# Order of VectorE's scores, sums, maxima and quantisation in a 16-head attention kernel

## What is computed

```python
xn = layernorm(x)                                   # over the last axis, no weights
q = heads(xn @ q_w.T + q_b) / 4;  k = heads(xn @ k_w.T + k_b);  v = heads(xn @ v_w.T + v_b)
ctx = softmax(q @ k.T) @ v                          # 16 heads, 4096 x 4096 scores each
attn = merge(ctx) @ out_w.T + out_b
ffn = ((fp8(xn * sx) @ fp8(w * sw).T) / (sx * sw) + bias).astype(bfloat16)   # e4m3, one scale each
out = x + attn + ffn
```

## Time and profile before

| | us |
|---|---|
| median of 3 runs (lowest, highest) | 2136.94 (2135.54, 2138.78) |
| profiled execution, its own time | 2133.51 |
| its span in the profile | 2131.7 |
| TensorE busy | 2010.7 |
| ScalarE busy | 1833.7 |
| VectorE busy | 1302.3 |
| mean granted TensorE clock | 0.973 of full |

### The profile page before, as it was taken

One profiled execution on the slowest core, in us unless ns is written; L12 is line 12 of the kernel. 1 busy time (PEld: TensorE's weight loads), 2 busy tenths in 40 slices (PEclk: granted clock), 3 DMA queues, 4 the chain that ended last, 5 costly groups with the idle time before them and its releaser, 6 DMA issues.

```text
span 2131.7 us, 39151 instructions
## 1 busy us (share of the span) xinstructions
PE 2010.7 (94%) x13433; PEld 661.4 (31%) x13433; DVE 1302.3 (61%) x1822; ACT 1833.7 (86%) x2004; POOL 32.2 (2%) x53
## 2 busy tenths in 40 slices
PE   6889999999999999999999999999999999999988
PEld 4523232322323232322323232222322232222327
DVE  6555566665555567655555667555555666565556
ACT  2259898998989898998989899998989899898973
POOL 2000000000000000000000000000000000000000
PEclk9989999999999999999999999999999999999999
DMA  6850201212020111111030111112020011111022
GB/s 204 265 193 9 42 10 15 27 23 28 13 37 8 30 14 20 28 22 28 8 42 8 17 26 22 28 23 28 8 42 8 15 27 23 28 21 29 8 38 80
DMA packets 65525, 82.12 MB, mean 39 GB/s; under 512 B 9952, under 2 KB 47360, under 8 KB 62208
## 3 DMA queue, kind: packets, MB, share of 16 engines
q1 hardware_dynamic: 65472, 81.58, 18.9%
HBM read 54.79 MB, written 26.21 MB: 38 GB/s over the span
## 4 chain that ended last, share of the span: by engine, by line
PE 74%; DVE 20%; issue 2%; DMA 2%; SPq 1%; ACT 0%; DVEq 0%; ACTq 0%
PE banks L1089 39%; PE banks L1063 29%; DVE d_probs L835 6%; DVE d_probs L831 3%; DVE bits L820 3%; DVE d_probs L838 2%; DVE bits L826 2%; PE banks L977 2%; DVE powers L823 2%; PE banks L1189 1%; PE banks L988 1%; PE banks L1021 1%; DMA k_parts<-probs 1%; DVE o_junk L640 1%; DVE qt L641 1%
## 5 line engine op out<-in xcount | busy, mean ns | idle before, releaser
L583 ACT ACTIVATE probs<-banks 128x1024 f32<-128x1024 f32 x1923 | 1783.1, 1179 | 159.2 <-PE banks L1063 154.4
L1089 PE MATMUL banks<-probs,v_st 128*32 128x512 f32 x7680 | 1036.8, 612 | 3.0 <-DVE o_sb L801 3.0
L1063 PE MATMUL banks<-q_st,k_st 50*128 50x512 f32 x4102 | 863.2, 471 | 25.3 <-DVE bits L820 18.9
L1063 PEld LDWEIGHTS banks<-q_st,k_st 50*128 50x128 f32 x4102 | 378.2, 186 | 1001.0 <-ACT probs L583 882.6
L835 DVE SCALAR_TENSOR_TENSOR d_probs<-d_probs,bits 128x1024 f32<-128x1024 f32 x256 | 313.6, 1225 | 8.8
L820 DVE TENSOR_SCALAR bits<-banks 128x512 int32<-128x512 f32 x256 | 177.1, 692 | 203.6 <-PE banks L1063 191.6
L1089 PEld LDWEIGHTS banks<-probs,v_st 128*32 128x32 f32 x7680 | 152.3, 108 | 291.1 <-issue 270.8
L801 DVE STREAM_TRANSPOSE o_sb<-banks 128x512 f32<-128x512 f32 x32 | 22.9, 717 | 357.3 <-PE banks L1089 357.3
L831 DVE SCALAR_TENSOR_TENSOR d_probs<-bits 128x1024 f32<-128x1024 f32 x128 | 156.9, 1225 | 13.0 <-PE banks L1089 9.8
L838 DVE SCALAR_TENSOR_TENSOR d_probs<-d_probs,powers 128x1024 f32<-128x1024 f32 x128 | 157.9, 1234 | 4.4
L826 DVE TENSOR_SCALAR bits<-bits 128x1024 int32<-128x1024 int32 x128 | 88.9, 695 | 4.4
(11 more groups left out here) (91 smaller groups left out, 483.4 us busy)
## 6 DMA issues: line engine op xcount, KB each, us to landing
k_st<-k_parts SPq DMA_DIRECT2D x204, 128.0 KB, 4.4
q_st<-q_parts SPq DMA_DIRECT2D x204, 64.0 KB, 5.1
q_parts<-probs SPq DMA_DIRECT2D x9, 512.0 KB, 6.1
k_parts<-probs SPq DMA_DIRECT2D x9, 512.0 KB, 6.2
xnT_copy<-probs SPq DMA_DIRECT2D x8, 512.0 KB, 4.4
probs<-xnT_copy SPq DMA_DIRECT2D x8, 512.0 KB, 8.0
w_f<-xnT_copy SPq DMA_DIRECT2D x16, 256.0 KB, 5.1
out_dram<-qt SPq DMA_DIRECT2D x16, 256.0 KB, 2.1
```

The lines of the kernel that those rows point to most:

```text
L583: act.activation(probs[:, at:at + WIDE * CHUNK].rearrange("p (t c) -> p t c", t=WIDE), banks[:, bank:bank + WIDE, :], ACT.Exp, scale=1.0 / ...
L1063: return pe.matmul(out, k_mm[rows, kt * P:(kt + 1) * P], blocks[rows, qb // GROUPS], start=True, stop=True)
L1089: last = pe.matmul(banks[VCOLS * qb:VCOLS * (qb + 1), 6, :], v_st[:, kt, :], tile, start=(pos == 0), stop=(pos == KT - 1), tile_position=( ...
```

## The change

It moves the slots of VectorE's scores and sums, puts a D row's sum behind the block's own sum of its round instead of between the round's two pairs, takes maxima over 32 keys (16 query tiles of 32 columns in one bank, made in two parts in slots 36 and 38 and reduced once), makes those scores from 48 rows instead of 16, moves the transposing matmul to slot 46, and puts quantisation behind the maxima on VectorE.

```diff
-    D_SLOTS = ((5, 6, 9, 16), (18, 25, 27, 34))
-    D_SUM = (26, 44)
+    D_SLOTS = ((2, 4, 6, 14), (16, 24, 26, 34))
+    D_SUM = (23, 43)
-    MAX_FIRST, MAX_TURN = 42, 47
+    MAX_SLOTS, MAX_TURN = (36, 38), 46
-    AK = 64
-    JT = CHUNK // AK
+    AK = CHUNK // UT
...
-                self.max_jobs = UT * (S // CHUNK) if full else UT // JT
+                self.max_jobs = UT * (S // CHUNK) if full else 1
...
-            if e in D_SUM:
-                SUM_ORDER.append((e, None, D_SUM.index(e), D_ROWS[D_SUM.index(e)]))
+            SUM_ORDER += [(e, None, d, D_ROWS[d]) for d in range(len(D_ROWS)) if D_SUM[d] == e]
...
-                def some_maxima(j, job0):
-
-                    dve.wait_ge(c.misc_full, job0 + (j + 1))
-                    dve.tensor_reduce(mcol[:, JT * j:JT * (j + 1)], misc.rearrange("p (t k) -> p t k", t=JT),
-                                      AX.X, ALU.max).then_inc(c.misc_free, 1)
+                def some_maxima(job):
+
+                    dve.wait_ge(c.misc_full, job + 1)
+                    dve.tensor_reduce(mcol[:, :], misc.rearrange("p (t k) -> p t k", t=UT), AX.X, ALU.max
+                                      ).then_inc(c.misc_free, 1)
...
+                    neg_count[0] = h * 2 + 3
+                    lk = lk + (MAX_LINKS + SUM_LINKS)
+                    maxima(job + QB * len(D_ROWS), lk)
                     if not c.full:
 
                         dve.wait_ge(xq_in, h * 16 + 16)
...
                         qstep(dve.tensor_tensor(two, two, bo_sb[:, :, :], ALU.add))
-                    neg_count[0] = h * 2 + 3
-                    lk = lk + (MAX_LINKS + SUM_LINKS)
-                    maxima(job + QB * len(D_ROWS), lk)
...
-                def max_job(u, j, job, ready=True):
-
-                    misc_job(job, ready)
-                    rows = slice(j * GROUP, j * GROUP + DH)
-                    for i in range(JT):
-                        at = u * UG + i * P
-                        last = pe.matmul(misc[:, i * AK:(i + 1) * AK], q_top[rows, at:at + P], k_top[rows, 0:AK],
+                def max_part(u, g, job, count, ready=True):
+
+                    if g == 0:
+                        misc_job(job, ready)
+                    else:
+                        pe.wait_ge(c.max_half, count)
+                    rows = slice(g * GROUP, g * GROUP + KROWS)
+                    for t in range(GT):
+                        at, to = u * UG + t * P, (g * GT + t) * AK
+                        last = pe.matmul(misc[:, to:to + AK], q_top[rows, at:at + P], k_top[rows, 0:AK],
                                          start=True, stop=True)
-                    last.then_inc(c.misc_full, 1)
+                    last.then_inc(c.misc_full if g == GROUPS - 1 else c.max_half, 1)
...
-                            for j in range(c.max_jobs):
-                                jobs[u * UE + MAX_FIRST + 2 * j] = (
-                                    lambda u=u, j=j: max_job(1 - u, j, job_of[u] + (D_JOBS + j)))
+                            for g, e in enumerate(MAX_SLOTS):
+                                jobs[u * UE + e] = lambda u=u, g=g: max_part(1 - u, g, job_of[u] + D_JOBS, h * 2 + (2 + u))
...
-                        if not c.full and e % UE == MAX_FIRST:
+                        if not c.full and e % UE == MAX_SLOTS[0]:
```

More of the change, by code:

```diff
@@ L227, in __init__ @@
                 self.row_ready = sem(f"{tag}_row_ready")
+                self.max_half = sem(f"{tag}_max_half")
                 self.chain = sem(f"{tag}_chain")
@@ L244, in program @@
         OUT_0 = 16
-        FIRST_MAX = {3: 0, 4: 1}
+        FIRST_MAX = (3, 4)
         TURN_FIRST = 5
@@ L268, in program @@
             SUM_ORDER += [(e, i, None, kt) for i, kt in enumerate(A_ROWS) if exp_of(QB * i + QB - 1) == e]
-            if e in D_SUM:
-                SUM_ORDER.append((e, None, D_SUM.index(e), D_ROWS[D_SUM.index(e)]))
-        SUM_OF_A = {i: pos for pos, (_, i, _, _) in enumerate(SUM_ORDER) if i is not None}
-        SUM_OF_D = {d: pos for pos, (_, _, d, _) in enumerate(SUM_ORDER) if d is not None}
+            SUM_ORDER += [(e, None, d, D_ROWS[d]) for d in range(len(D_ROWS)) if D_SUM[d] == e]
+        WHOLE = [(i, d) for _, i, d, _ in SUM_ORDER]
+        SUM_OF_A = {i: pos for pos, (i, _) in enumerate(WHOLE) if i is not None}
+        SUM_OF_D = {d: pos for pos, (_, d) in enumerate(WHOLE) if d is not None}
         def ring_user(tile):
@@ L767, in maxima @@
                     else:
-                        for j in range(c.max_jobs):
-                            some_maxima(j, job0)
+                        some_maxima(job0)
                         dve.wait_ge(c.misc_free, job0 + c.max_jobs)
                     minus_maxima(job0 + c.max_jobs, link0)
-                def some_maxima(j, job0):
-                    dve.wait_ge(c.misc_full, job0 + (j + 1))
-                    dve.tensor_reduce(mcol[:, JT * j:JT * (j + 1)], misc.rearrange("p (t k) -> p t k", t=JT),
-                                      AX.X, ALU.max).then_inc(c.misc_free, 1)
+                def some_maxima(job):
+                    dve.wait_ge(c.misc_full, job + 1)
+                    dve.tensor_reduce(mcol[:, :], misc.rearrange("p (t k) -> p t k", t=UT), AX.X, ALU.max
+                                      ).then_inc(c.misc_free, 1)
                 def minus_maxima(job, link0):
@@ L861, in attend @@
                         remainders(NCH + n, n % 2, 1, (1,))
-                        if n in FIRST_MAX:
-                            some_maxima(FIRST_MAX[n], 0)
+                        if n == FIRST_MAX[-1]:
+                            some_maxima(0)
                         if n < 4:
@@ L1071, in d_scores, with weighted_sum @@
                     score_tile(misc, D_ROWS[d], u, qb).then_inc(c.misc_full, 1)
-                def weighted_sum(h, u, pos):
-                    e, i, d, kt = SUM_ORDER[pos]
-                    if pos == 0:
+                def weighted_sum(h, u, n):
+                    e, i, d, kt = SUM_ORDER[n]
+                    first_one, last_one = n == 0, n == len(SUM_ORDER) - 1
+                    if first_one:
                         pe.wait_ge(c.acc_free, h * 2 + (u + ACC_0))
@@ L1080, in weighted_sum @@
                         pe.wait_ge(c.exp_done, h * HE + (EXP_0 + u * UE + exp_of(QB * i + QB - 1) + 1))
+                        for qb in range(QB):
+                            at = (u * UT4 + QB * i + qb) % RING * CHUNK
+                            last = pe.matmul(banks[VCOLS * qb:VCOLS * (qb + 1), 6, :], v_st[:, kt, :],
+                                             probs[:, at:at + CHUNK], start=first_one, stop=last_one,
+                                             tile_position=(0, VCOLS * qb))
                     else:
                         pe.wait_ge(c.d_ready, h * (UNITS * len(D_ROWS) * 2) + (u * len(D_ROWS) + d + 1) * 2)
[L1083 to L1090, removed]
+                        for qb in range(QB):
+                            last = pe.matmul(banks[VCOLS * qb:VCOLS * (qb + 1), 6, :], v_st[:, kt, :],
+                                             d_probs[:, qb * CHUNK:(qb + 1) * CHUNK], start=False,
+                                             stop=False, tile_position=(0, VCOLS * qb))
                     last.then_inc(c.pv_done, 1)
@@ L1105, in attend @@
                         if n in FIRST_MAX:
-                            j = FIRST_MAX[n]
-                            if j == 0:
+                            g = FIRST_MAX.index(n)
+                            if g == 0:
                                 pe.wait_ge(c.q_in[0], LOADS)
@@ L1110, in attend @@
                                 pe.wait_ge(v_done, V_0 + 2 * NCH)
-                            max_job(0, j, j, ready=j > 0)
+                            max_part(0, g, 0, 1, ready=False)
                 JOB0 = c.max_jobs + 1
@@ L1148, in attend @@
                             jobs[e]()
-                        for pos in range(KT):
-                            if SUM_ORDER[pos][0] == e % UE:
-                                weighted_sum(h, u, pos)
+                        for n, entry in enumerate(SUM_ORDER):
+                            if entry[0] == e % UE:
+                                weighted_sum(h, u, n)
                 pe.wait_ge(c.exp_done, EXP_0 + HEADS * HE + LEAD)
```

## The result

The changed kernel takes **1986.71 us** (median of 4, 1980.12 to 1989.21) against 2137.41: a ratio of 0.9291, 95% interval 0.9265 to 0.9316, so 150.7 us less. The forecast was 2012 with a range of 1992 to 2046: right in direction and in where the time went, too small by 25 us, and outside its range. The profiled execution took 1988.86 with a span of 1987.0.

What follows compares the result with a forecast made beforehand. ScalarE's exponentials were the floor, 1765.8 us; 32 units losing 1.40 each (44.8) and 1.0 at the start made 1811.6, 124.9 less than 1936.5, so 2008.6 profiled and 2012 as median. Range 1992 to 2046.

Steps and rivals of the forecast that it cites:

- step 1: End of unit 1: quantisation behind the maxima removes TensorE's wait for VectorE, 45.7 us in sum, and the low clock.
- step 2: Single scores' new slots: slot 25's old wait goes, 18.9 us in 32 units; slots 14 and 34 have 0.3 us margin.
- the transposing matmul's round: Slots 46 and 47, transposing matmul between the pairs: round taken as 2.10 us, losing 0.08.
- hidden lag of 0.65: All rounds: TensorE may fall 0.65 us behind before ScalarE loses time.
- Step 3 and 4, the D sum's 1.00: Slots 23 and 43: a D sum adds 1.00 us to its round, of which 0.35 and 0.64 are lost.
- Step 4, the maxima rounds' 2.20: Slots 36 and 38: maxima rounds stay at 2.20 us, each adding 0.36 lag, 0.23 lost; lower end 1.66.
- The last one's own 1.03: ScalarE's pace: a run of 40 exponentials, 36.86 us less the last one's 1.03, over 39 intervals: 0.9187 each.
- rival B: All units: more is hidden, only D sums lose, 0.35 and 0.25; 1986 us; sign: exponentials in runs of 60; chance 0.12.
- A: Slots 14 and 34 or D sums: order too tight, every unit loses 2.77 us; 2056 us; chance 0.13.
- C: Attention overflows with the shift from 32 keys and is done again; 3950 us or more; chance 0.02.
- D: Slot 36 of unit 1: the k load lands late; some 2140 us; chance 0.01.
- E: End of unit 1: the change does not work and VectorE's stall stays; 2083 us; chance 0.03.

Runs made afterwards that it cites:

- experiment 1: Kernel before with only VectorE's maxima put ahead of quantisation in unit 1; 2051.3 us, ratio 0.9605.
- experiment 4: Changed kernel with the D sums in slots 24 and 44, between the round's two pairs; 2007.88 us.
- Experiments 3 and 7: 3: changed kernel with maxima from 16 rows instead of 48, 2001.29 us; 7: experiment 1's kernel with 48 rows instead of 16 in its maxima jobs, 2041.26 us.
- a_moved: Changed kernel with later slots: singles 16, 26, 28, 36, uncut D sums 23 and 45, maxima 38 and 40, transposing matmul 49; 1979.65 us.
- a_turn47: Changed kernel with the transposing matmul in slot 47, behind the second pair, instead of 46; 1983.23 us.
- a_rows16: Changed kernel with maxima made from 16 rows of q and k instead of 48; 2001.29 us.

## Why the prediction was wrong, and where it was right
Right, by its own steps: the floor is ScalarE; step 1's stall went with the order (experiment 1), and its low clock with it; the wait of slot 25 went (step 2), neither slot 14 nor 34 brought one; the transposing matmul's round was 2.11 for 2.10; no k load was late and no overflow came. The hidden lag of 0.65 held: at slot 23, 0.85 - 0.24 = 0.61.

Wrong were two terms of the sum, the same mechanism with other sizes:
- **Step 3 and 4, the D sum's 1.00.** It was taken from a sum that follows a maxima job (544.93 - 543.93); alone between two pairs one adds 1.20 (experiment 4). Behind another sum it adds 0.85. With 0.85, slot 23's stretch is 0.30 instead of 0.45; measured 0.34.
- **Step 4, the maxima rounds' 2.20**, and "48 rows instead of 16 have the same columns to stream: nothing". Experiments 3 and 7 show that the rows are worth 0.2 us a round; measured 1.96. With 1.96, 0.85 and a pace of 0.9166, the lag at slot 43 is 0.26 - 0.17 + 0.85 = 0.94, of which 0.29 is lost, and the end comes to about 0.38 instead of 0.95; measured 0.42. In the forecast's own sum this term weighs more: it takes 0.48 off a unit, the D sum's 0.30.

The pace was also a little off. "The last one's own 1.03" is a misreading, since the last of a run of 40 lasts 1.47; taking off 1.03, which is what the first one lasts, gives the distance of the ends by luck. And 0.08 of it isn't pace but a loss early in each run of 40.

In us: 31 units with 0.65 less loss are 20 less; the pace by ends, 0.9166 instead of 0.9187, is 4 less; the first unit lost 7.5 instead of 2.4, 5 more. That is the 19 us between 1811.6 and 1792.6. The other 6 lie in the runs: the profiled execution stood 3.4 below the median before and 2.1 above it after. The range failed with it: its lower end came from rival B by a cut of half, though B's mechanism, D sums alone losing, was nearly what happened; the maxima round's lower end, 1.66, was named and then not carried into the range. That B's 1986 is the measured time is luck: by its terms first to last exponential is 1786.0 and not 1792.6, and the 6 us of the runs make up for it. B's sign, runs of 60 exponentials, came too, but such runs hide losses, so it was no sign of B alone.

Rivals A, C, D and E didn't occur. The stall that A looked for in two margins of 0.3 us can't be seen in any unit.

## What to carry to other kernels
Price a round by the distance between starts, with its neighbours in the place where it will stand: a sum behind a sum, a job with about as many rows as the scores and a wait all cost something else than their own rows say. Small losses hide below the idle times of merged rows, so compare ends of instructions and whole units. And before growing an unrolled loop on an engine, look at the fetch queue: some 65 fulfilled waits cost more than half of this change's gain.

## What the runs showed that was not expected
- Instruction fetches at a loop's return: 15 standstills of up to 4.8 us and 135 to 136 further fetches of 16 KB, once TensorE's loop has 1834 instructions, and none at 1769.
- The start of attention. TensorE's granted clock there, in the changed kernel:
```profile
148.00:152.00 4.00, 4.00 (x21) 0.85 (x20) 3.81 (x4) 2.50 (x4) 0.00 (x0) 0.50 0.00 0
```
It stays at 1.2 GHz until about 154, though TensorE is busy from 136 on; in the kernel before it was at 2.4 GHz from 141. The first unit loses about 5 us more by it: it takes 62.6 us here and 61.8 and 62.5 in a_moved and a_turn47, whose clock rose at 152, but 57.3 in a_rows16, where it rose at 142. What decides it stays open. It may be behind the runs' spread of 9 us: the fastest, 1980.12, has a mean granted clock of 0.993, the other three 0.990. This wasn't tried.
- A matmul of 16 rows between others of 50 costs 0.2 us more for a group of eight than one of 48, at 32 columns and at 64.
